# Second attention of a two-layer kernel: who normalises the first three groups, who adds the second group, who copies the mask constants

## The reference

```python
x = x + jnp.tanh(g_xattn[0]) * _L0_xattn_ref(_layernorm(x, axis=-1), ctx_1024, ...)
x = x + jnp.tanh(g_ffn[0]) * _L0_ffn_ref(_layernorm(x, axis=-1), ...)
x = x + jnp.tanh(g_xattn[1]) * _L1_xattn_ref(_layernorm(x, axis=-1), ctx_1024, ctx_1024, mask_BxS2_bk1, ...)
x = x + jnp.tanh(g_ffn[1]) * _L1_ffn_ref(_layernorm(x, axis=-1), ...)
# _layernorm: (x - mean) / sqrt(var + eps);  _L1_xattn_ref:
Qp = q @ Wq + bq
qk = jnp.einsum('bqd,bkd->bqk', Qp, Kp) + mask[:, None, :].astype(qk.dtype)
attn = jax.nn.softmax(qk, axis=-1)
out = jnp.einsum('bqk,bkd->bqd', attn, Vp)
```

## Time and profile before

| | us |
|---|---|
| median of 3 runs | 860.49 |
| the three runs | 856.09, 860.49, 864.86 |
| the profiled execution | 855.35 |
| its span | 853.6 |
| mean granted TensorE clock | 0.921 of full speed |
| busy in the span: PE, DVE, ACT, POOL | 696.7, 720.7, 595.1, 580.8 |

### The profile page before, as it was taken

The page is one execution under the profiler, slowest core; times in us unless marked ns, Lnnn a source line. Parts: engine busy times, 40 slices in busy tenths (PEclk is TensorE's granted clock), DMA queues, the critical chain, the costliest instruction groups (busy, mean ns, idle before and its releaser), DMA issues. The chain is left out here.

```text
span 853.6 us, 19514 instructions
## 1 busy us (share of the span) xinstructions
PE 696.7 (82%) x6608; PEld 539.2 (63%) x6608; DVE 720.7 (84%) x1821; ACT 595.1 (70%) x1210; POOL 580.8 (68%) x561
## 2 busy tenths in 40 slices
PE   5988879999999989898989989999926879256535
PEld 2767657787877767776768777777723657122234
DVE  3999998989898999776998777778736999799988
ACT  4667657777877766477767767777746888399856
POOL 4675458888888788855577777765558992388810
PEclk9899989999999999799999999999966999666659
DMA  9421812323334122835697877878749622000005
GB/s 247 129 101 54 149 70 97 118 89 116 111 113 144 53 101 102 270 104 187 213 298 236 286 256 270 264 261 276 240 138 303 207 89 74 16 0 1 0 28 170
DMA packets 89665, 127.66 MB, mean 150 GB/s; under 512 B 19888, under 2 KB 64512, under 8 KB 83424
## 3 DMA queue, kind: packets, MB, share of 16 engines
q1 hardware_dynamic: 80016, 108.00, 39.9%
q0 software_dynamic: 8672, 17.99, 6.0%
q10 hardware_dynamic: 880, 0.43, 0.2%
HBM read 82.76 MB, written 43.53 MB: 148 GB/s over the span
## 5 line engine op out<-in xcount | busy, mean ns | idle before, releaser
L531 POOL DMA_INDIRECT m_results<-a_probs,e_to x142 | 147.1, 1036 | 58.0 <-issue 36.3
L521 POOL DMA_INDIRECT m_tokens_to<-r_rows,r_place x128 | 132.2, 1033 | 51.0 <-issue 31.2
L540 POOL TENSOR_TENSOR a_probs<-a_probs,a_top 128x1024 f32<-128x1024 f32 x64 | 122.1, 1908 | 55.3 <-DVE a_top L1512 54.5
L750 ACT ACTIVATE room<-a_ps_s,e_bias 128x512 f32<-128x512 f32 (+1 forms) x160 | 102.0, 646 | 52.6 <-PE a_ps_s L1053 47.2
L658 ACT ACTIVATE a_probs_t<-a_ps_pt 128x512 f32<-128x512 f32 x128 | 69.2, 591 | 65.4 <-PE a_ps_pt L956 65.4
L1542 DVE TENSOR_TENSOR e_hp<-room,e_hp 128x512 fp32r<-128x512 f32 (+1 forms) x160 | 103.2, 645 | 5.5
L1540 DVE CAST e_hp<-room 128x512 fp32r<-128x512 f32 (+1 forms) x160 | 67.7, 423 | 42.1 <-ACT room L750 29.6
L1477 DVE TENSOR_TENSOR a_probs<-a_ps_s,a_mask 128x1024 f32<-128x1024 f32 x64 | 77.9, 1217 | 7.1 <-PE a_ps_s L841 6.6
L940 PEld LDWEIGHTS a_ps_o<-a_vals,a_probs_t 128*64 128x64 f32 x2048 | 66.4, 139 | 21.1 <-issue 20.4
L1512 DVE TENSOR_REDUCE a_top<-a_probs 128x16 f32<-128x1024 f32 x64 | 77.2, 1206 | 0.2
L1049 PE MATMUL a_ps_s<-e_xt,e_weights 128*128 128x512 f32 (+1 forms) x160 | 65.2, 407 | 10.7 <-DMA e_weights<-m_weights_to 10.7
(11 more groups left out here) (366 smaller groups left out, 1928.2 us busy)
## 6 DMA issues: line engine op xcount, KB each, us to landing
e_weights<-m_weights_to SPq DMA_DIRECT2D x40, 1024.0 KB, 4.9
m_weights_to<-r_parts SPq DMA_DIRECT2D x8, 1024.0 KB, 5.7
room<-m_tokens_to SPq DMA_DIRECT2D x31, 264.0 KB, 4.1
c_two<-m_results SPq DMA_DIRECT2D x3, 1536.0 KB, 12.0
a_ctx_in<-in_ctx_dram SPq DMA_DIRECT2D x17, 256.0 KB, 3.7
m_keys_t<-n_keys SPq DMA_DIRECT2D x16, 256.0 KB, 2.2
m_values<-n_values SPq DMA_DIRECT2D x16, 256.0 KB, 3.0
out_dram<-x_sb SPq DMA_DIRECT2D x15, 256.0 KB, 2.3
```

Of the source, the lines that this page charges most:

```text
L521: pool.indirect_dma_start(tokens_to, bass.IndirectOffsetOnAxis(ap=place[:, k, q:q + 1], axis=0), rows[:, c % RING, q % CT, k, :], None).th ...
L531: pool.indirect_dma_start(results, bass.IndirectOffsetOnAxis(ap=to[:, v, r:r + 1], axis=0), y[:, v, r], None).then_inc(returned[v], 16)
L540: pool.tensor_tensor(probs[:, j], probs[:, j], top[:, j].unsqueeze(2).broadcast_to([P, HEADS, SEQ]), ALU.subtract).then_inc(shifted, 1)
L750: act.activation(h[:, c, at], ps_h[c][:, at], ACT.Gelu_apprx_tanh, bias=bias[:, n % ROWS, c:c + 1]).then_inc(h_sb, 1)
```

## The change

Four edits are made at the seam of the first two blocks.

- Group 0, 1 and 2 are normalised by VectorE with four `tensor_scalar` (subtract the mean, multiply by the reciprocal) where ScalarE had four activations; the small VectorE instruction that prepared their bias (L1673, L2026) goes.
- Group 1's sums go from the end of VectorE's list in the first block to the end of GpSimd's list in that block.
- The copy of `term_k` to `more_terms` goes from the head of VectorE's list in the second block to the head of ScalarE's.
- ScalarE's two one-column warming activations (L1860, L1862) go, and `evict_q(1)` moves ahead of `roots(3)`.

```diff
@@ GpSimd, first block
         pool.wait_ge(terms, 12)
+        pool.wait_ge(two_in[1], 16)
+        pool.tensor_tensor(two[:, 1, :, 0], two[:, 1, :, 0], two[:, 1, :, 1], ALU.add).then_inc(f_pool, 1)
+        pool.wait_ge(f_pool, 1)
+        pool.tensor_tensor(x_sb[:, QUAD:2 * QUAD], x_sb[:, QUAD:2 * QUAD], two[:, 1, :, 0], ALU.add).then_inc(f_pool, 1)
@@ ScalarE, first block
         act.activation(f_std[:], f_mv[:, :, 1], ACT.Sqrt, bias=power[:, 0, 0:1]).then_inc(f_std_ready, 1)
-        act.wait_ge(f_nmr_ready, 1)
-        for k in range(QUAD):
-            act.activation(xn[:, 0, k], x_sb[:, k], ACT.Identity, scale=f_rstd[:, k:k + 1], bias=f_nmr[:, k:k + 1])\
-                .then_inc(f_xn_ready, 1)
@@ VectorE, first block
         dve.reciprocal(f_rstd[:], f_std[:]).then_inc(f_rstd_ready, 1)
         dve.wait_ge(f_rstd_ready, 1)
-        dve.scalar_tensor_tensor(out=f_nmr[:], in0=f_mv[:, :, 0], scalar=-1.0, in1=f_rstd[:],
-                                 op0=ALU.mult, op1=ALU.mult).then_inc(f_nmr_ready, 1)
-        first_sums(1)
+        for k in range(QUAD):
+            dve.tensor_scalar(xn[:, 0, k], x_sb[:, k], f_mv[:, k, 0:1], f_rstd[:, k:k + 1], ALU.subtract, ALU.mult)\
+                .then_inc(f_xn_ready, 1)
@@ ScalarE, second block
-        act.activation(warm[:], tg[:, 0:1], ACT.Square).then_inc(warmed, 1)
-        act.wait_ge(warmed, 1)
-        act.activation(warm[:], warm[:], ACT.Sqrt).then_inc(warmed, 1)
...
+        act.wait_ge(ahead_in, 96)
+        act.activation(more_terms[:], term_k[:], ACT.Copy).then_inc(terms_copied, 1)
         evict_x(0)
         roots(1)
-        normalise(1)
-        act.wait_ge(ahead_in, 96)
         evict_q(0)
         evict_x(1)
         roots(2)
-        normalise(2)
+        evict_q(1)
         roots(3)
...
-            if s + 1 < SUPERS:
+            if 1 <= s < SUPERS - 1:
                 evict_q(s + 1)
@@ VectorE, second block
-        def less_mean(n):
+        def normalise(n):
             dve.wait_ge(rstd_ready, n)
-            dve.scalar_tensor_tensor(out=nmr[:, tiles(n)], in0=mv[:, tiles(n), 0], scalar=-1.0, in1=rstd[:, tiles(n)],
-                                     op0=ALU.mult, op1=ALU.mult).then_inc(nmr_ready, 1)
-
-        dve.wait_ge(ahead_in, 96)
-        dve.tensor_copy(more_terms[:], term_k[:]).then_inc(terms_copied, 1)
-        for n in range(1, NORMALISED_BY_ACT):
+            if n >= 2:
+                dve.wait_ge(xt_ps, n - 1)
+            for k in range(QUAD):
+                t = n * QUAD + k
+                last = dve.tensor_scalar(xn[:, n % 2, k], x_sb[:, t], mv[:, t, 0:1], rstd[:, t:t + 1],
+                                         ALU.subtract, ALU.mult)
+            last.then_inc(xn_first, 1)
+
+        for n in range(1, NORMALISED_BY_DVE):
             rows_of(n)
             factors(n)
-            less_mean(n)
+            normalise(n)
         rows_of(3)
         rows_of(4)
```

More of the change, by code:

```diff
@@ L163, in layer0_and_experts @@
     f_rows, f_mv = stats[:, 0:QUAD], mv[:, 0:QUAD]
-    f_std, f_rstd, f_nmr = (n[:, 0:QUAD] for n in (rstd2, rstd, nmr2))
+    f_std, f_rstd = (n[:, 0:QUAD] for n in (rstd2, rstd))
     f_warm = bias_rest[0:1, 127:128]
@@ L1654, in _ @@
             dve.tensor_scalar(w[:, n], w[:, n], MAGIC - 127.0, MAGIC + 127.0, ALU.max, ALU.min).then_inc(w_dve, 1)
-        def first_sums(n):
-            four = slice(n * QUAD, n * QUAD + QUAD)
-            dve.wait_ge(two_in[n], 16)
-            dve.tensor_tensor(two[:, n, :, 0], two[:, n, :, 0], two[:, n, :, 1], ALU.add).then_inc(f_summed, 1)
-            dve.wait_ge(f_summed, n + 1)
-            dve.tensor_tensor(x_sb[:, four], x_sb[:, four], two[:, n, :, 0], ALU.add).then_inc(f_added, 1)
-        first_sums(0)
+        dve.wait_ge(two_in[0], 16)
+        dve.tensor_tensor(two[:, 0, :, 0], two[:, 0, :, 0], two[:, 0, :, 1], ALU.add).then_inc(f_summed, 1)
+        dve.wait_ge(f_summed, 1)
+        dve.tensor_tensor(x_sb[:, 0:QUAD], x_sb[:, 0:QUAD], two[:, 0, :, 0], ALU.add).then_inc(f_added, 1)
         dve.wait_ge(f_added, 1)
@@ L1878, in evict_q @@
             act.activation(q[:], ps_q[:].rearrange("p a b -> p (a b)"), ACT.Identity, bias=bq[:, 0:1]).then_inc(q_sb, 1)
-        def normalise(n):
-            act.wait_ge(nmr_ready, n)
-            if n >= 2:
-                act.wait_ge(xt_ps, n - 1)
-            for k in range(QUAD):
-                t = n * QUAD + k
-                last = act.activation(xn[:, n % 2, k], x_sb[:, t], ACT.Identity, scale=rstd[:, t:t + 1], bias=nmr[:, t:t + 1])
-            last.then_inc(xn_first, 1)
+        act.wait_ge(ahead_in, 96)
+        act.activation(more_terms[:], term_k[:], ACT.Copy).then_inc(terms_copied, 1)
         evict_x(0)
         roots(1)
-        normalise(1)
-        act.wait_ge(ahead_in, 96)
         evict_q(0)
```

20 lines of the change are left out of this document (9 added, 11 removed).

## The result

The changed kernel takes 865.51 us (median of 22 runs, 859.20 to 870.72) against 856.34 us before (22 runs): ratio 1.0106, 95% interval 1.0087 to 1.0126. It is slower by about 9 us (7.4 to 10.8). The forecast was 859.5 with a range up to 864.0, and 1.0 us faster than the kernel before, so it was wrong in sign and size. The starting value was also high: the forecast was counted from 860.49, the median of three runs, and 22 runs give 856.34. The profiled execution after takes 860.96 us with a span of 859.2. All ratios leave out executions more than 1.5% above the fastest of their kernel, among them one of 1340.96 us in `d2_vector_adds_third`.

What follows compares the result with a forecast made beforehand. The seam was bound by ScalarE's last arrival, the second block's head by GpSimd's unbroken list, later steps by VectorE. Gains of 0.4 (seam) and 0.6 (second block) made 1.0 us: 860.49 to 859.5, range 855.5 to 864.0.

Steps and rivals of the forecast that it cites:

- the last arrival goes from 641.75 to 641.4: End of the first block: the last engine finishes earlier, 0.4 us gained (lower bound 0, upper 0.9).
- sized at 0.5 to 0.9 us: Estimate for four 128x128 `tensor_scalar` on VectorE; 0.55 us was taken, against 1.65 on ScalarE.
- The cost of 1.77 us from last arrival to release: Seam of the first two blocks: the second block starts 1.77 us behind ScalarE, the last to arrive.
- GpSimd's second sum holds VectorE until R + 2.65, and four `tensor_scalar` end at R + 3.2: Second block's head, R being its release: group 1 is normalised by R + 3.2, before at about R + 5.6.
- if the four stood apart by 1.3 us each: Sign of being wrong, second block's head: the four `tensor_scalar` spaced by 1.3 us, not one block of 0.5 to 0.9.
- The forecast's reason against turns: Runs of four `tensor_scalar`: nothing is between the four, and each is over in 0.1 to 0.2 us.
- GpSimd is delayed by 0.9 us: Second block: VectorE's two runs of four keep GpSimd's unbroken list out for 0.9 us (bounds 0 and 1.1).
- The rival "take turns": Second block: a waiting GpSimd instruction precedes each of VectorE's four; 1.9 us slower in all, 862.4 us, chance 0.15.
- a clock that rises much later: Sign of being wrong: TensorE's clock, 0.50 in 643 to 653, rising much earlier or later than before the change.
- The forecast's 0.6 for the second block: Second block: GpSimd's 1.53 us wait at 684.06 vanishes, less its 0.9 delay, so the stage ends 0.6 us earlier.
- no case reaches one per cent: Whole kernel: no case reaches 8.6 us; within one per cent 0.95, faster 0.03, slower 0.02.

Runs made afterwards that it cites:

- d2_vector_adds_third: Kernel before with ScalarE's part of the change alone, plus group 2's two sums in the second block moved from GpSimd to VectorE: ratio 0.9949 to the kernel before.
- a1_gpsimd_adds: Kernel before with one edit: GpSimd, not VectorE, makes group 1's sums at the end of the first block; ratio 1.0023 to the kernel before.
- b1_early_drain: Changed kernel plus a GpSimd drain behind its constants, ahead of its wait for group 1's results; ratio 1.0076 to the kernel before.
- b2_vector_adds: Changed kernel with VectorE again making group 1's sums in the first block; ratio 1.0038 to the kernel before.

## Why the prediction was wrong

**The seam.** The step that failed is "the last arrival goes from 641.75 to 641.4". It took the end of GpSimd's last sum, 640.85, for GpSimd's arrival. An engine arrives when its closing drain has ended, and GpSimd's first one behind this block's indirect DMAs ends 3.83 us behind its work. That drain was in the trace before, at 635.0, ending at 638.83 with nothing to wait for; hidden cover of this kind was not looked for. Forecast 0.4 us gained, measured 3.04 lost. GpSimd alone makes it (`a1_gpsimd_adds`), an early drain removes nearly all of it, and so does taking the sums away but for 0.6 us (`b1_early_drain`, `b2_vector_adds`). The gain of 0.4 isn't there even so: VectorE's four `tensor_scalar` of group 0, sized at 0.5 to 0.9 us, take 1.89 (1.98 in `b1_early_drain`, whose seam is 6.97 for 6.81 before). The cost of 1.77 us from last arrival to release was right.

**The four `tensor_scalar`.** The step that failed is "GpSimd's second sum holds VectorE until R + 2.65, and four `tensor_scalar` end at R + 3.2". It held the four as one burst behind one wait. They ended at R + 6.45, one sum of GpSimd between each two. This is the forecast's own sign of being wrong ("if the four stood apart by 1.3 us each"). The forecast's reason against turns, that nothing stands between the four, counts for nothing: a waiting GpSimd instruction goes ahead all the same. The row of the one that had come in between two VectorE instructions was the evidence, and it was read as depending on the semaphore there. The duration itself was also low: 1.11 us without a neighbour, for an estimate of 0.5 to 0.9.

The Trainium skill, page "SBUF — State Buffer", section "Who interferes with whom", says that the shared ports are held for the length of one instruction by whoever issues first. The traces agree: four small instructions waited four times (4.30 us), two wide ones twice (2.67) and, in their second run, once (2.37).

**GpSimd is delayed by 0.9 us.** Wrong sign of the effect: its ten sums start at 644.15 and end at 657.02, 12.87 us, where they took 12.94 before. VectorE's four go into its gaps at no cost to it; VectorE pays alone. Behind the sums GpSimd then waits 2.94 us for a reciprocal that VectorE has not come to.

**The rival "take turns"** had the mechanism, its place and its first steps right (groups normalised at R + 6.9 and R + 13.3: measured R + 6.45 and R + 12.94; first maximum to end at R + 16: R + 15.6). It was sized wrongly behind them. It put the roots of 5 to 7 at R + 23.6 where VectorE goes on at R + 26.23, and so 2.3 us for a measured 4.99. The forecast gave it a chance of 0.15. The 4.9 us by which VectorE goes on later are what the block loses: from that point to the third block before and after take 69.26 and 69.36, and 69.25 to 69.58 in all runs but the two with ScalarE's part alone, where VectorE has no wait at that point (70.28). The 4.9 us have two parts. At the first exponentials the block is 3.32 us late; that is the turns. On the way from there to the table load, which starts at R + 24.6 (before R + 19.7), another 1.57 us come of TensorE's products at the lower clock. No rival of the forecast had this part. The forecast only named a clock that rises much later as a sign of being wrong, and it rose at R + 15.6 for R + 10.4.

**ScalarE's part** was worth its place: the copy and the order of the evictions gain 0.82 us alone. The forecast's 0.6 for the second block counted this part together with the normalising, which alone costs 5.37.

**That no case reaches one per cent** failed because the two errors add: 3.04 + 4.99, with only gains or one loss of 1.9 foreseen.

## What to carry to other kernels

At a point where all engines meet, read the end of each sequencer's closing instruction, not of each engine's last piece of work, and before giving an engine something to do late in a block ask whether it now has idle time there that hides such an instruction. Beside an engine whose list has no gap, a run of small VectorE instructions on SBUF costs about one of the neighbour's durations for each (four took four here, eight took six), not one wait plus the short times. Make it few wide instructions, which then hold up the neighbour as well, or leave it to ScalarE, even if that takes longer by itself (1.65 us here for 1.11). A wait that disappears is worth nothing if the same engine must first get through the work that was moved to it. And a lateness can grow behind its cause: ask whether TensorE now stands idle longer ahead of products that others wait for, and read the granted clock there.
